# Attention stage: norm parts in other half units, weighing between score tiles where no projection stands, and the loop over images written out

## The chip, the cores and the metric

The kernel runs on one core of a Trainium2 chip. The metric is the device time of one execution in microseconds (us). Five engines matter: PE (TensorE, matmul), DVE (VectorE), ACT (ScalarE), POOL (GpSimd) and SP (SyncE, which here issues every DMA).

## What is computed

The input is 8 images of 384 channels and 32 x 32 pixels. Three stages follow one another: a correlation and 1x1 convolution, an attention over the 1024 pixels of each image, and a feed-forward net. Only the attention is touched:

```
t = t + _L1_attn_ref(_ln_t(t), Wq, Wk, Wv, Wo, bo)

q, k, v = (x @ W.T) split into H = 12 heads of HD = 32
scores  = einsum('bhqd,bhkd->bhqk', q, k) * HD ** -0.5
probs   = softmax(scores, axis=-1)
out     = einsum('bhqk,bhkd->bhqd', probs, v)
return out @ Wo.T + bo
```

`_ln_t` takes mean and variance of a pixel's 384 channels. Weights and activations of the projections are split into two f16 parts (high and low), and a projection is nine matmuls for three products of parts.

## The kernel before, in words

**Order.** `attention_stage` writes one program for each engine, by hand. An image has 24 units (`IU`). Unit u of image b handles one group of 4 heads, a block of 256 queries (x = u // 2) and one half of the keys (kh = u % 2). It has two half units, e = 0 and 1. In a half, PE does four score tiles of 128 x 512 (`scores`, L903), one for each head, into two PSUM banks that alternate; ACT takes the exponential of each (`exponential`, L1237). Tile n waits for exponential n - 2. POOL adds each head's two exponentials of a unit (`add_pair`, L1367). PE then weighs: `weigh` (L934) multiplies the values with the exponentials (16 matmuls of f32) and sums the pairs with a matrix of ones (8 matmuls). It is called behind the fourth tile, and at e = 0 weighs the second half of the unit two before, at e = 1 the first half of the unit before.

**Maxima.** A wave (`wave`, L919) is four row-tiled matmuls into `mx`, four PSUM banks that exist once; DVE reduces it (`take_wave`, L1075). There is one wave at the end of each half, eight waves ahead of its use. After each fourth wave DVE builds the shifts of a block (`top`, `top_turned`, four `shift`), and SP sends them into a row of `qst` (`load_rows`, L764), for which the first score tile of the block waits.

**Beside this**, units 6 to 23 (`FIRST` = 6) of image b hold the 18 projections of image b + 1 (`project`, `project_part`), in pieces of the nine matmuls between the tiles, into one bank `pj`; ACT and DVE stage the results (`stage_high`, `stage_low`). In units 0 to 5 stand the six output projections of image b - 1 (`out_project`, `out_part`, `move_out`, POOL's `add`). When a block's sums are complete, ACT moves them out (`move_pv`), DVE inverts them in three steps (`invert_sum`) and multiplies (`attended`), and ACT and POOL split the result in two.

**Norm** of image b + 2, in units 6 to 23 with `load`: POOL folds (`fold_x`, units 8, 9), PE takes the mean (`mean`, units 10 and 11 = `MEAN_AT`), DVE centres three times for each half of the image (`centre`), ACT squares and POOL folds in units 12 to 15, PE takes the variance (`var`, units 16 and 17 = `VAR_AT`), DVE turns it (`invert_std` step 0), POOL raises it to -0.5 (`invert`), DVE turns it back (step 2) and scales (`normalise`). The two f16 parts are made in units 0 to 2 of the next image (`z_high` on ACT, `z_low` on DVE). `beside(n)` on ACT and DVE says after which exponential, or place n of 8, a part stands; on DVE the waves are taken ahead of n = 0 and 4. A mean or variance matmul uses `pj`, so the units `MEAN_AT + VAR_AT` (10, 11, 16, 17) have their whole projection in the first half, and unit 3 has it in the second.

**Schedule.** `schedule` (L688) gives the order over images. Units 0 to 5 of image 0 stand ahead of a hardware loop `Fori(0, last - 1)` of six turns; its body is units 6 to 23 of image b and units 0 to 5 of image b + 1. Behind it are written out: units 6 to 23 of image 6 (no load) and all of image 7 (units 6 to 23 without projections). SP has the same loop (L811); at the end of its body it waits for the last `add`, stores the image and loads the residual of the next (L818 to L820), ahead of the shifts' rows of the next unit 6.

## Time and profile before

| | |
|---|---|
| median of 3 runs | 2930.32 us (2927.63 to 2931.25) |
| the profiled execution | 2929.51 us |
| its span, first to last instruction | 2927.6 us |
| mean granted TensorE clock | 0.951 |
| PE, busy matmul | 2624.0 us, 90% |
| DVE | 1849.9 us, 63% |
| ACT | 1533.7 us, 52% |
| POOL | 1418.2 us, 48% |
| attention stage, first to last exponential | 474 to 2087 us |
| DMA packets | 68634, 164.41 MB |

Matmuls are pipelined, and a busy share is a mean over three stages with other limits. So what counts here is the attention stage by units: how long a unit takes, which engine is busy for all of it, and where PE stands idle, with the engine that released it. PEclk is the granted clock as a share of 2.4 GHz; 0.5 is 1.2 GHz.

### The profile page before, as it was taken

The numbers are of one execution on the slowest core, as the hardware profiler recorded it, in microseconds if no ns is written. First come the engines' busy times: TensorE is split into PE (matmuls) and PEld (weight loads), VectorE is DVE, ScalarE is ACT, GpSimd is POOL, SyncE is SP. The second block draws the span as 40 slices with busy tenths as digits, with TensorE's granted clock in tenths as the row PEclk, the third lists the DMA queues.
The fourth block names the chain that finished last, engine by engine and source line by source line (L and its number), as shares of the span: only waits on it lengthen the run. The fifth ranks groups of instructions, "written<-read, shape, count | busy, mean of one in ns | idle before, by whom it ended". The sixth has DMA issues, their size and how long they took to land. (4 is left out here: it accounts for less than half of the span.)

```text
span 2927.6 us, 64485 instructions
## 1 busy us (share of the span) xinstructions
PE 2624.0 (90%) x23600; PEld 1287.3 (44%) x23600; DVE 1849.9 (63%) x2359; ACT 1533.7 (52%) x2602; POOL 1418.2 (48%) x1113
## 2 busy tenths in 40 slices
PE   4989756998998998998899999998679999999999
PEld 3555323444453443444444444543234444444444
DVE  6766347887887887797887887777243333333332
ACT  2333124666666665665666666666444444444443
POOL 2333054777776776777766777677511111111010
PEclk8889878999999999999999999999989999999999
DMA  4233132111212112112112112120111010101010
GB/s 153 82 117 110 67 122 84 52 31 50 77 31 95 36 36 92 39 31 96 32 42 96 30 30 74 31 73 2 40 69 43 22 44 21 43 21 43 21 43 22
DMA packets 68634, 164.41 MB, mean 56 GB/s; under 512 B 13569, under 2 KB 17470, under 8 KB 67326
## 3 DMA queue, kind: packets, MB, share of 16 engines
q1 hardware_dynamic: 68350, 160.60, 17.3%
q8 instruction: 181, 2.97, 0.4%
q14 instruction: 103, 0.84, 0.1%
HBM read 59.13 MB, written 37.75 MB: 33 GB/s over the span
## 5 line engine op out<-in xcount | busy, mean ns | idle before, releaser
L1372 POOL TENSOR_TENSOR b_pair<-b_ex 128x512 f32<-128x512 f32 x768 | 979.8, 1301 | 440.4 <-ACT b_ex L1244 439.2
L1244 ACT ACTIVATE b_ex<-b_st 128x512 f32<-128x512 f32 x1536 | 860.3, 597 | 463.6 <-PE b_st L913 445.7
L1079 DVE TENSOR_REDUCE b_mxp<-b_mx 128x4 f32<-128x2048 f32 x384 | 876.6, 2283 | 222.2 <-PE b_mx L929 208.2
L913 PE MATMUL b_st<-b_qst,b_kst 97*128 97x256 f16 (+1 forms) x3072 | 541.3, 280 | 58.8 <-ACT b_ex L1244 35.8
L1628 DVE TENSOR_TENSOR c_gs<-c_g,c_gs 128x512 f16<-128x512 f32 x192 | 132.7, 692 | 481.9 <-ACT c_gs L1701 481.9
L946 PE MATMUL b_pv<-b_ex,b_v 128*32 128x256 f32 x6144 | 420.7, 392 | 0.0
L1549 PE MATMUL c_hid<-c_z,c_wi 128*128 128x512 f16 x1728 | 405.3, 380 | 11.3 <-DVE c_z L1621 11.3
L1564 PE MATMUL c_acc<-c_gs,c_wo 128*128 128x512 f16 x1728 | 404.0, 379 | 0.3 <-DVE c_gs L1628 0.3
L913 PEld LDWEIGHTS b_st<-b_qst,b_kst 97*128 97x128 f16 (+1 forms) x3072 | 226.3, 98 | 367.2 <-ACT b_ex L1244 203.9
L1697 ACT ACTIVATE c_g<-c_hid,c_bias 128x512 f32<-128x512 f32 x192 | 131.3, 684 | 363.6 <-PE c_hid L1549 363.4
L1549 PEld LDWEIGHTS c_hid<-c_z,c_wi 128*128 128x128 f16 x1728 | 169.3, 98 | 227.5 <-issue 19.0
L1564 PEld LDWEIGHTS c_acc<-c_gs,c_wo 128*128 128x128 f16 x1728 | 169.0, 98 | 204.4 <-ACT c_gs L1701 0.8
L1734 POOL TENSOR_TENSOR c_xs<-c_x 128x512 f32<-128x512 f32 x16 | 21.9, 1367 | 477.3 <-DMA c_x<-after_attention 475.0
L954 PE MATMUL b_pv<-b_pair,b_ones 128*32 128x256 f32 x3072 | 240.3, 385 | 0.8 <-POOL b_pair L1372 0.8
L946 PEld LDWEIGHTS b_pv<-b_ex,b_v 128*32 128x32 f32 x6144 | 162.6, 110 | 153.2 <-issue 85.3
L929 PE MATMUL b_mx<-b_kst,b_qst 32*128 32x512 f16 x1536 | 153.4, 389 | 77.6 <-DVE b_mxp L1079 75.8
L929 PEld LDWEIGHTS b_mx<-b_kst,b_qst 32*128 32x128 f16 x1536 | 38.7, 91 | 241.5 <-issue 125.3
L873 PE MATMUL b_pj<-b_z,b_wq 128*128 128x512 f16 x405 | 123.9, 402 | 18.3 <-DVE b_z L1062 11.4
L954 PEld LDWEIGHTS b_pv<-b_pair,b_ones 128*32 128x32 f32 x3072 | 101.2, 112 | 70.2 <-issue 5.0
L1701 ACT ACTIVATE c_gs<-c_g 128x512 f16<-128x512 f32 x192 | 120.9, 629 | 6.1
L897 PE MATMUL b_pj<-b_ao,b_wo 128*128 128x512 f16 x432 | 119.6, 379 | 4.5 <-ACT b_ot L1264 4.5
L308 PE MATMUL a_conv<-a_fs,a_wm 128*128 128x512 f16 x432 | 117.4, 423 | 0.0
(169 smaller groups left out, 2758.5 us busy)
## 6 DMA issues: line engine op xcount, KB each, us to landing
a_x<-in_x SPq DMA_DIRECT2D x8, 1536.0 KB, 6.7
a_ob<-a_x SPq DMA_DIRECT2D x8, 1536.0 KB, 7.1
after_conv<-a_ob SPq DMA_DIRECT2D x24, 512.0 KB, 2.6
b_xl<-after_conv SPq DMA_DIRECT2D x8, 1536.0 KB, 7.3
b_qst<-b_staged0q SPq DMA_DIRECT2D x192, 64.0 KB, 2.0
b_kst<-b_staged0k SPq DMA_DIRECT2D x192, 64.0 KB, 2.0
b_v<-b_vstaged SPq DMA_DIRECT2D x24, 512.0 KB, 3.0
b_xr<-after_conv SPq DMA_DIRECT2D x8, 1536.0 KB, 6.6
```

The lines of the kernel that those rows point to most:

```text
L873: last = nc.tensor.matmul(bank[:, :], ws[kind][a][:, k, g * P:(g + 1) * P], z[b][:, k, part * BANK:(part + 1) * BANK], start=n == 0, stop= ...
L913: last = nc.tensor.matmul(st[n % NST][:, j * QUERIES:(j + 1) * QUERIES], kst[g][0:depth, s, kt * P:(kt + 1) * P], qst[g][0:depth, s, q0:q0 ...
L929: last = nc.tensor.matmul(mx[:, s, :], qst[g][rows, s, q0 + t * P:q0 + (t + 1) * P], kst[g][rows, s, half * BANK:(half + 1) * BANK], start ...
L946: last = nc.tensor.matmul(pv[s * HEAD:(s + 1) * HEAD, 0:QUERIES], v[g][:, kt, s * HEAD:(s + 1) * HEAD], ex[u % 2][e][s][:, j * QUERIES:(j ...
L954: last = nc.tensor.matmul(pv[s * HEAD:(s + 1) * HEAD, QUERIES:BANK], ones[:, :], pair[u % 2][s][:, e * QUERIES:(e + 1) * QUERIES], start=F ...
L1079: nc.vector.reduce_max(mxp[x % 2][:, w // 2, :, w % 2], mx[:, :, :], AX_X).then_inc(mx_taken, 1)
L1244: nc.scalar.activation(ex[u % 2][e][s][:, :], st[n % NST][:, :], ACT.Exp, scale=SCALE).then_inc(exp_ready, 1)
L1372: nc.gpsimd.tensor_tensor(pair[u % 2][s][:, :], ex[u % 2][0][s][:, :], ex[u % 2][1][s][:, :], ALU.add).then_inc(pair_ready, 1)
L1549: last = nc.tensor.matmul(hid[m % NH][:, :], wi[a][:, k, m * P:(m + 1) * P], z[p][b][:, k, :], start=n == 0, stop=n == 8)
L1564: last = nc.tensor.matmul(acc[j][:, :], wo[a][:, m, j * P:(j + 1) * P], gs[m % NS][b][:, :], start=m == 0 and n == 0, stop=m == MC - 1 and ...
L1628: nc.vector.tensor_tensor(gs[m % NS][1][:, :], g[m % NG][:, :], gs[m % NS][0][:, :], ALU.subtract).then_inc(glo_ready, 1)
L1697: nc.scalar.activation(g[m % NG][:, :], hid[m % NH][:, :], ACT.Gelu, bias=bias[:, m:m + 1], scale=1.0 / WSCALE).then_inc(gelu_ready, 1)
```

## The change

On PE, DVE, ACT, POOL and SP the loop over images becomes a loop of the program's text, so that each image is written out. `mean` and `centre` of half 1 move to unit 13, its matmul to the first half unit; which half holds a whole projection is now in `WHOLE` (unit 10: first, 11 and 13: second, 16 and 17: first; 3: second as before). `weigh` is cut in two, `weigh_values` and `weigh_sums`; in a half without a projection the values stand behind the second score tile and the sums behind the third. The steps of `invert_std`, `normalise`, `z_low` and `z_high`, POOL's `invert` and `stage_low` of odd units get other places.

```diff
--- before.py
+++ after.py
@@ -691,7 +691,7 @@
             prologue()
             for u in range(FIRST):
                 unit(0, u, out_proj=False, norm=True)
-            with eng.Fori(0, last - 1) as b:
+            for b in range(last - 1):
                 for u in range(FIRST, IU):
                     unit(b, u, load=True)
                 for u in range(FIRST):
@@ -720,7 +720,10 @@
             return ot if in_prologue(m) else std_turned
 
         V_UNITS = [FIRST + 6 * g + 4 + part for g in range(GROUPS) for part in range(2)]
-        MEAN_AT, VAR_AT = V_UNITS[0:2], V_UNITS[2:4]
+        VAR_AT = V_UNITS[2:4]
+        MEAN_AT = ((V_UNITS[0], 1), (V_UNITS[1] + 2, 0))
+        WHOLE = {V_UNITS[0]: 0, V_UNITS[1]: 1, V_UNITS[1] + 2: 1, VAR_AT[0]: 0, VAR_AT[1]: 0}
+        CENTRE_FROM = (5, 1)
 
         def has_wave(b, h):
             return not (isinstance(b, int) and b == n_images - 1 and h + AHEAD >= WAVES)
@@ -808,7 +811,7 @@
             prologue()
             for u in range(FIRST):
                 unit(0, u)
-            with sp.Fori(0, last - 1) as b:
+            for b in range(last - 1):
                 for u in range(FIRST, IU):
                     unit(b, u)
                     if u == FIRST:
@@ -931,7 +934,7 @@
                                             start=True, stop=True, tile_position=(s * HEAD, 0))
                 last.then_inc(mx_ready, 1)
 
-            def weigh(b, u, e):
+            def weigh_values(b, u, e):
                 x, kh = u // 2, u % 2
                 unit_no = IU * b + u
                 g = x // 4
@@ -949,7 +952,10 @@
                                                 start=kt == 0, stop=False,
                                                 tile_position=(0, s * HEAD))
                 last.then_inc(pv_ready, 1)
-                pe.wait_ge(pair_ready, HG * (unit_no + 1))
+
+            def weigh_sums(b, u, e):
+                kh = u % 2
+                pe.wait_ge(pair_ready, HG * (IU * b + u + 1))
                 for s in range(HG):
                     last = nc.tensor.matmul(pv[s * HEAD:(s + 1) * HEAD, QUERIES:BANK], ones[:, :],
                                             pair[u % 2][s][:, e * QUERIES:(e + 1) * QUERIES],
@@ -986,41 +992,45 @@
                     part = lambda n0, n1: out_part(b - 1, u, n0, n1)
                 if u == FIRST:
                     free[id(pj)] = None
-                first_half = qkv and u in MEAN_AT + VAR_AT
-                second_half = u == KC
+                whole = 1 if u == KC else WHOLE.get(u)
 
                 for e in range(2):
                     scores(b, u, e, 0)
                     scores(b, u, e, 1)
+                    if load and (u, e) in MEAN_AT:
+                        mean(b + 2, MEAN_AT.index((u, e)))
                     pieces = (0, 0), (0, 0)
-                    if first_half or second_half:
-                        if e == second_half:
-                            pieces = (0, 5), (5, 9)
-                    else:
+                    if begin and whole is None:
                         pieces = ((0, 3), (3, 5)) if e == 0 else ((5, 8), (8, 9))
-                    if begin and pieces[0][1]:
+                    elif begin and e == whole:
+                        pieces = (0, 5), (5, 9)
+                    weighed = lagging(b, u, 2 - e) and (*before(b, u, 2 - e), 1 - e)
+                    if pieces[0][1]:
                         if pieces[0][0] == 0:
                             if u == FIRST:
                                 pe.wait_ge(exp_ready, FILLS * (IU * b + u) + 1)
                             begin()
                         part(*pieces[0])
-                    if load and u in MEAN_AT and e == 1:
-                        mean(b + 2, MEAN_AT.index(u))
+                    elif weighed:
+                        weigh_values(*weighed)
                     if load and u in VAR_AT and e == 1:
                         var(b + 2, VAR_AT.index(u))
                     scores(b, u, e, 2)
-                    if begin and pieces[0][1]:
+                    if pieces[0][1]:
                         part(*pieces[1])
+                    elif weighed:
+                        weigh_sums(*weighed)
                     scores(b, u, e, 3)
-                    if lagging(b, u, 2 - e):
-                        weigh(*before(b, u, 2 - e), 1 - e)
+                    if weighed and pieces[0][1]:
+                        weigh_values(*weighed)
+                        weigh_sums(*weighed)
                     if has_wave(b, 2 * u + e):
                         wave(b, 2 * u + e)
 
             def epilogue(b):
-                weigh(b, IU - 2, 1)
-                weigh(b, IU - 1, 0)
-                weigh(b, IU - 1, 1)
+                for u, e in ((IU - 2, 1), (IU - 1, 0), (IU - 1, 1)):
+                    weigh_values(b, u, e)
+                    weigh_sums(b, u, e)
                 for i in range(6):
                     out_project(b, i)
                     out_part(b, i, 0, 9)
@@ -1113,6 +1123,8 @@
                 dve.wait_ge(sum_inverted, INVERSE * (BLOCKS * b + x + 1))
                 nc.vector.tensor_tensor(pvs[:, 0:QUERIES], pvs[:, 0:QUERIES], inv[:, :], ALU.mult
                                         ).then_inc(att_ready, 1)
+
+            NORMALISE = ((18, 6), (19, 1), (19, 2), (20, 6), (21, 1), (22, 5))
 
             def prologue():
                 nc.vector.memset(top[:, :], 0.0).then_inc(const_set, 1)
@@ -1161,26 +1173,24 @@
             def unit(b, u, out_proj=True, norm=True, qkv=True, load=False):
                 def beside(n):
 
-                    if n == 5 and u >= FIRST and qkv:
-                        stage_low(b + 1, u - FIRST)
                     if u % 2 == 0 and n == 1 and lagging(b, u, 4):
                         attended(b, (u - 4) // 2)
-                    if load and u in MEAN_AT and n >= 5:
-                        centre(b + 2, MEAN_AT.index(u), n - 5)
-                    if load and u == VAR_AT[0] and n >= 5:
-                        invert_std(b + 2, 0, n - 5)
-                    if load and (u, n) in ((VAR_AT[1], 5), (VAR_AT[1], 7), (VAR_AT[1] + 1, 2)):
-                        invert_std(b + 2, 1, (5, 7, 2).index(n))
-                    if load and (u, n) in ((18, 3), (18, 6), (19, 1)):
-                        normalise(b + 2, 0, (3, 6, 1).index(n))
-                    if load and (u, n) in ((19, 2), (20, 6), (21, 1)):
-                        normalise(b + 2, 1, (2, 6, 1).index(n))
+                    for h in range(HALVES):
+                        k = n - CENTRE_FROM[h]
+                        if load and u == MEAN_AT[h][0] and 0 <= k < KC:
+                            centre(b + 2, h, k)
+                    if load and (u, n) in ((VAR_AT[0], 5), (VAR_AT[1], 5)):
+                        invert_std(b + 2, 0, 2 * (u - VAR_AT[0]))
                     if u % 2 and n >= 5 and lagging(b, u, 3):
                         invert_sum(b, (u - 3) // 2, n - 5)
-                    if norm and (u, n) in ((0, 6), (0, 7), (1, 1)):
-                        z_low(b + 1, 0, (6, 7, 1).index(n))
-                    if norm and (u, n) in ((1, 7), (2, 2), (2, 3)):
-                        z_low(b + 1, 1, (7, 2, 3).index(n))
+                    if n == (7 if u % 2 else 5) and u >= FIRST and qkv:
+                        stage_low(b + 1, u - FIRST)
+                    if load and (u, n) in ((VAR_AT[1], 7), (VAR_AT[1] + 1, 5)):
+                        invert_std(b + 2, 1, 2 * (u - VAR_AT[1]))
+                    if load and (u, n) in NORMALISE:
+                        normalise(b + 2, *divmod(NORMALISE.index((u, n)), KC))
+                    if norm and u < 2 * KC and n == (1 if u % 2 else 5):
+                        z_low(b + 1, u // KC, u % KC)
 
                 for n in range(8):
                     if n % 4 == 0 and has_wave(b, 2 * u + n // 4 - 1):
@@ -1299,9 +1309,9 @@
                         h, step = u // 2 - 6, u % 2
                         if n in (1, 5) and (step == 0 or n == 1):
                             square(b + 2, h, 2 * step + n // 5)
-                    if norm and u < 2 and n in (1, 3, 5):
-                        z_high(b + 1, u, n // 2)
-                    if qkv and u >= FIRST and n == (2 if u in MEAN_AT + VAR_AT else 6):
+                    if norm and u in (0, 2, 4) and n in (1, 5):
+                        z_high(b + 1, *divmod(u + n // 5, KC))
+                    if qkv and u >= FIRST and n == {None: 6, 0: 3, 1: 7}[WHOLE.get(u)]:
                         stage_high(b + 1, u - FIRST)
                     if u % 2 and n == 3 and lagging(b, u, 3):
                         move_pv(b, (u - 3) // 2)
@@ -1401,8 +1411,8 @@
                 for s in range(HG):
                     if load and u in (8, 9) and s == 1:
                         fold_x(b + 2, u - 8)
-                    if load and (u, s) in ((VAR_AT[0], 3), (VAR_AT[1], 3)):
-                        invert(b + 2, VAR_AT.index(u))
+                    if load and s == 0 and u - 1 in VAR_AT:
+                        invert(b + 2, VAR_AT.index(u - 1))
                     if load and 12 <= u < 16 and s == 3 - u % 2 * 2:
                         fold_square(b + 2, u // 2 - 6, 1 + u % 2)
                     if u % 2 == 0 and s == 3 and lagging(b, u, 4):
```

## Rows read from the trace of the kernel before

**Rows 1.** Waits: engine and line, what it waited for: us, times, longest.

```profile
PE b_mx L929 <- DVE b_mxp L1079: 75.8, 37, 5.8
```

**Rows 2.** Busy us by stretch (columns in the first line); cut at units' first exponentials.

```profile
core 0: us, PE busy (x) PEld busy (x) DVE busy (x) ACT busy (x) POOL busy (x), PEclk, DMA share, GB/s
679.19:709.20 30.01, 24.36 (x245) 11.20 (x244) 25.01 (x26) 17.76 (x33) 23.21 (x19) 0.94 0.21 56
...
716.68:738.50 21.82, 18.18 (x164) 7.84 (x163) 12.34 (x16) 10.75 (x20) 12.98 (x12) 0.84 0.38 143
1757.64:1773.49 15.85, 15.30 (x165) 7.26 (x164) 13.04 (x16) 10.76 (x21) 13.20 (x12) 1.00 0.26 101
761.75:795.53 33.78, 32.45 (x384) 17.25 (x383) 28.77 (x37) 22.58 (x43) 24.93 (x22) 1.00 0.14 41
810.75:863.73 52.98, 48.45 (x546) 25.38 (x545) 46.12 (x59) 32.03 (x61) 40.17 (x31) 0.97 0.16 41
1844.57:1892.09 47.52, 46.22 (x543) 23.98 (x542) 37.23 (x47) 32.00 (x61) 31.64 (x28) 1.00 0.17 46
1628.67:1636.15 7.48, 7.48 (x83) 3.46 (x81) 7.13 (x12) 5.94 (x12) 6.20 (x6) 1.00 0.01 4
1829.30:1836.93 7.63, 7.63 (x83) 3.59 (x82) 7.15 (x12) 5.12 (x10) 4.96 (x5) 1.00 0.01 1
1970.96:2060.62 89.66, 74.09 (x865) 31.54 (x864) 68.03 (x85) 56.86 (x109) 61.83 (x54) 1.00 0.01 2
474.29:522.36 48.07, 36.57 (x360) 14.44 (x360) 39.15 (x46) 30.10 (x58) 29.72 (x24) 0.86 0.04 14
```

**Rows 3.** Timeline of PE, units 5 and 6 of image 1: start, us, line, [idle <-releaser].

```profile
726.38 0.61 PE L913 MATMUL b_st<-b_qst,b_kst 97*128 97x256 f16 x4 [2.58 <-issue]
```

**Rows 4.** Timeline of PE, end of unit 17's first half, image 1.

```profile
825.87 0.39 PE L929 MATMUL b_mx<-b_kst,b_qst 32*128 32x512 f16 x4 [2.64 <-DVE b_mxp L1079]
```

**Rows 5.** Timeline of DVE: image 0 unit 2, image 1 unit 17, image 6 unit 2.

```profile
495.63 1.29 DVE L1062 TENSOR_TENSOR b_z<-b_xl,b_z 128x512 f16<-128x512 f32 x2
...
822.92 0.71 DVE L1050 STREAM_TRANSPOSE b_xs<-b_std_col 128x512 f32<-128x512 f32 x1 [4.10 <-POOL b_std_col L1364]
...
1733.94 3.44 DVE L1062 TENSOR_TENSOR b_z<-b_xl,b_z 128x512 f16<-128x512 f32 x2
```

**Rows 6.** Timeline of POOL: the power for unit 17 of image 1.

```profile
819.97 2.92 POOL L1364 TENSOR_TENSOR b_std_col<-b_std_col,b_power 128x16 f32<-128x16 f32 x1
```

**Rows 7.** Groups by line: busy us, mean ns of one | idle before.

```profile
L1079 DVE TENSOR_REDUCE b_mxp<-b_mx 128x4 f32<-128x2048 f32 x384 | 876.6, 2283 | 222.2 <-PE b_mx L929 208.2 <-issue 13.1
```

**Rows 8.** Timeline of PE, first scores of unit 14: in the loop, written out.

```profile
1628.24 0.61 PE L913 MATMUL b_st<-b_qst,b_kst 97*128 97x256 f16 x4
...
1828.79 0.61 PE L913 MATMUL b_st<-b_qst,b_kst 97*128 97x256 f16 x4
```

**Rows 9.** Timeline of ACT, first exponentials of the same two units.

```profile
1628.67 1.08 ACT L1244 ACTIVATE b_ex<-b_st 128x512 f32<-128x512 f32 x2 [1.00 <-PE b_st L913]
...
1829.30 2.41 ACT L1244 ACTIVATE b_ex<-b_st 128x512 f32<-128x512 f32 x4 [1.00 <-PE b_st L913]
```

**Rows 10.** Timeline of PE, one half unit of the last image.

```profile
2000.33 0.61 PE L913 MATMUL b_st<-b_qst,b_kst 97*128 97x256 f16 x4
2001.49 0.88 PE L913 MATMUL b_st<-b_qst,b_kst 97*128 97x256 f16 x4 [0.55 <-ACT b_ex L1244]
2002.30 1.07 PE L946 MATMUL b_pv<-b_ex,b_v 128*32 128x256 f32 x16
2003.19 0.61 PE L954 MATMUL b_pv<-b_pair,b_ones 128*32 128x256 f32 x8
```

**Rows 11.** Timeline of PE, start of unit 8 of image 6.

```profile
1781.26 0.61 PE L913 MATMUL b_st<-b_qst,b_kst 97*128 97x256 f16 x4 [0.58 <-DMA b_qst<-b_shift]
```

**Rows 12.** DMA queue of instructions: packets, MB; 1098 to 1306 us, then 1750 to 1958.

```profile
q8 instruction: 20, 0.33, 0.7%
...
q8 instruction: 18, 0.29, 0.6%
```

## The prediction

> **What bounds the kernel now.** I read the attention stage alone (474 to 2087 us of the span): the diff touches nothing else. A unit is one pass of the inner order: eight score tiles and exponentials, four pair sums, two waves (the row maxima of a later block, in `mx`, one buffer, emptied by DVE). First the windows by stretch [rows 2], each cut at a unit's first exponential: a steady unit is 7.48 us with PE busy for all of it, so PE bounds it. What exceeds that stands in three places of each image. (1) Units 5 and 6, where the loop over images turns: 21.82 us, against 15.85 where the same units are written out (image 6). (2) Units 1 to 3: 30.0 us. (3) Units 16 to 21: 52.98, against 47.52 in image 6, which loads nothing and so has no norm parts there. Then the waits [rows 1]: PE's wave matmul waits for DVE's reduce, 75.8 us in all. In time order: at the turn PE stands still for 2.58 us with "issue" as the reason [rows 3], so nothing of the program holds it, and the window's clock is 0.84 against 1.00, which makes up the rest of the 6 us. In unit 17 PE waits 2.64 us for a reduce [rows 4]; DVE came late to it because it had waited 4.10 us for POOL's power [rows 5], which took 2.92 us and had been queued behind pair sums [rows 6]. In unit 2 DVE does two `z_low` in a row, 3.44 us [rows 5], between two reduces. Last, the last image: no projection from unit 6 on, and still 89.66/12 = 7.47 us a unit, since the third score tile starts 1.16 us after the first, behind exponential 0 [rows 10].
>
> **Part 1, the loop written out.** Removed: five turns. Each costs 21.82 - 15.85 = 5.97 us [rows 2]; by the same windows the five come to 29. **-29.** Added: straight-line code has its price in rows too. Where units are written out today (images 6, 7), unit 14 takes 7.63, not 7.48 [rows 2]: exponential 0 starts 0.51 us behind the first score matmul (1828.79 to 1829.30) instead of 0.43 (1628.24 to 1628.67) [rows 8, 9], PE's third tile waits for it, twice a unit. I charge +0.15 to each ordinary unit newly written out: units 8, 9, 14, 15, 22, 23 of images 0 to 5, 36 x 0.15 = **+5.4**, and units 0, 4, 5 of images 1 to 6, **+2.7**. A turn also gave the DMAs time. SP stores the image, loads the residual and only then sends the rows of shifts that unit 8 reads; in image 6 PE waits 0.58 us for them [rows 11], beside the 0.15: some 0.8 for unit 7, **+4** for images 1 to 5. No other engine's order changes by this part.
>
> **Part 2, norm parts.** `z_low` goes from units 0 to 2 to one in each of units 0 to 5, `z_high` with it on ACT. DVE's budget for a pair of units there: four reduces at 2.28 [rows 7] 9.1, the shift chain and `attended` 1.8, `invert_sum` 1.2, two `z_low` at 1.4 (between 0.65 alone and 1.72 beside POOL [rows 5]): 14.9 of 15.3. No stretch between two reduces holds more than 1.8, and a reduce may be 1.1 late before PE's next wave waits (half unit 3.8, less 0.4 of wave matmul, less 2.3). So lateness stays inside that cover: I take 0.3 us an image, between 0 and the 6 that are lost today. Units 1 to 3 of images 1 to 6 become 7.63 + 7.63 + 8.0 + 0.3 = 23.6 from 30.0 (six such stretches): 6 x -6.5 = **-39**. (8.0: unit 3 has a half without projection, below.)
> Units 16, 17: DVE's second transpose of the deviation moves from n 7 to n 5 of the next unit, and POOL's power to the head of units 17 and 18. POOL then has about 3 us from the end of the power to DVE's step; that wait goes. What is late next is DVE itself: behind unit 17's second reduce it has the transpose 0.7, `invert_sum` 1.2 and the next transpose and add 1.2, 3.1 us where 1.5 keep pace, and then two or three `normalise` and `stage_low` in 18 to 20. Going from reduce to reduce by hand, PE waits 0.15, 0.35, 0.7, 0.2, 0.3 and 0.4: 2.1 us (bounds 0 and the 5.4 of today). POOL's load in 17 and 18, 5.1 of pair sums, 0.3 and 2.9 each, is 8.3 against 8.9 and 8.0: its pair sums are read a unit later, which hides 0.3. Units 16 to 21: 47.52 as in image 6, written out already [rows 2], + 0.8 for the wait behind the two variance halves (part 3) + 2.1 = 50.4 from 52.98, 6 images: **-15.5**.
> Mean and centre of half 1 move from unit 11 to 13, unit 11 projects in its second half and waits no longer for the centring to free `pj`; unit 13 becomes whole and longer by 1.1. Units 10 to 13: unit 11 loses 1.0 and unit 12 0.4, unit 13 gains 1.1: 33.4 from 33.78 [rows 2], 6 images: **-2**.
> `stage_low` behind `invert_sum` in odd units: nothing, `pj` is asked for 2 us later.
>
> **Part 3, weighing between score tiles** where a half has no projection. In order of PE today such a half is: two tiles, idle until exponential 0, tile, tile, values 0.89 (2002.30 to 2003.19), sums and wave 0.88 [rows 10]: 3.74. Values and sums now fill the idle time: PE's own work is 0.44 + 0.22 + 0.22 + 0.89 + 0.88 and some 0.35 for four changes between f32 and f16, 3.0. But behind tile 3 only the wave and one tile stand ahead of the next half's tile 1, which shares its bank: 0.77 of work against 0.51 + 0.60 + 0.04 for exponential 3, so 0.38 of waiting comes back. A half is 3.4, a unit 6.8 (floor 6.6, the ring through the exponential; ceiling today's 7.47). DVE, 12 us of busy work and 0.5 of gaps a pair, allows 6.5. Last image, units 8 to 19: 12 x 6.8 = 81.6 from 89.66; units 20 to 23 and 3 together -0.7: **-8.7**. Units 6 and 7 there gain nothing, the rows of shifts end them. In the halves with a mean or a variance matmul (0.9) the idle time is already filled, and the order costs them 0.3 by that same wait; that is in the sums above, as is 0.35 gained in units 11 and 3. Image 6, no load: **-1**. Image 0, units 0 to 5: all halves are free, DVE bounds: twelve reduces 27.4, six `z_low` 9, chains 6, gaps 1.5 and the half clock at the start give 45 from 48.07 [rows 2]: **-3**.
>
> **Sum**: -29 + 5.4 + 2.7 + 4 - 39 - 15.5 - 2 - 8.7 - 1 - 3 = -86. The profiled execution took 2929.5 us (span 2927.6 and 1.9 around it): 2843.5. The median of the runs shown is 2930.3, 0.8 above; I forecast **2844**.
>
> **A rule weighed against the trace.** `z_low` is 0.65 in a stretch where POOL has nothing to do, and 1.72 a piece beside pair sums [rows 5]. The Trainium skill (SBUF — State Buffer, on the shared port pair) says that a DVE instruction with two SBUF inputs and a GpSimd instruction that reads SBUF exclude each other: the later one is blocked to the end of the earlier. By that rule a spread `z_low`, always beside a busy POOL, could take up to 1.3 + 0.65 us, and this speaks against the change; by it the sum would be some 10 us higher.
>
> **Rivals.** (A) *DVE remains late*: the spread parts add up, PE waits as long as today. For it: DVE's budget is 97% full in units 0 to 5, the 3.1 us in unit 17. Against it: the longest stretch between two reduces falls from 5.3 (chain and two `z_low`) to 3.1. Time: 2844 + 6 x (6.2 + 3.3) = 2900. (B) *The straight-line price is not paid*, because PE has work ahead in more halves or ACT's waits come out differently: 2844 - 8 - 12 = 2824. (C) *Port*: each `z_low` and `normalise` as long as 1.95: 6 x 1.7 = +10, 2854. (D) *Slower: instructions are not there in time.* Every instruction of five more images comes from memory once. If straight-line PE code stood still for 2.58 us, as at a turn, at each packet of the instruction queue (20 an image in the loop, 18 written out [rows 12]), 5 x 18 pauses would give +232, 3076; at the full 6 us it decides from 15 pauses on. Against it: the loop fetches as many packets today, and images 6 and 7 show 7.63 from unit to unit with no such pause. The Trainium skill (Runtime: NRT & Kernel Launch, Instruction fetch mechanics) says the same: sequential fetch is mostly hidden, a taken branch is not. (E) *No effect*: the gain of the turns is eaten by the row wait in unit 7 (up to 4 us each) and all stalls remain: 2925.
>
> **Chances.** Forecast's case (2820 to 2866) 0.72; A 0.12; B 0.06; C 0.05; D 0.03; E 0.02. Range: down to B, 2820; up by the stalls at half of today's (+28), and the last image unchanged (+8): 2880. Some 0.2% (6 us) is what a measurement can tell: faster 0.95, same 0.02, slower 0.03.
>
> **What would show it.** Right: no "issue" gap of over 1 us on PE between units 5 and 6, and the clock at 1.00 from image 1 to 7; units 1 to 3 near 23.6; no wait of DVE for POOL's power; unit 14 at 7.63; last image's units at 6.8. Wrong: PE's wait for the reduces still above 30 us; pauses named "issue" in straight code; unit 7 above 9.

## The result and the profile after

The changed kernel takes **2832.18 us**, median of 4 runs (2831.3 to 2832.55), the kernel before 2930.78 (2927.63 to 2934.43) beside it: a ratio of 0.9663, 95% interval 0.9646 to 0.9679. The forecast was 2844, range 2820 to 2880, faster: direction, range and most of the size hold. The profiled span fell from 2927.6 to 2830.6 us, by 97.

First the page after: span, busy time by engine, granted clock (PEclk), the instruction queue q8.

```profile
span 2830.6 us, 59176 instructions
...
PE 2625.7 (93%) x23600; PEld 1264.5 (45%) x23600; DVE 1845.6 (65%) x2359; ACT 1539.8 (54%) x2602; POOL 1420.7 (50%) x1113
...
PEclk8899868999999999999999999999799999999999
...
q8 instruction: 163, 2.67, 0.4%
```

The work is the same (PE 2625.7 us busy, 2624.0 before; DVE 1845.6 and 1849.9). Only idle time and clock differ.

Then the windows of after by stretch, cut at units' first exponentials (columns in the first line), each to be laid beside one of [rows 2].

```profile
core 0: us, PE busy (x) PEld busy (x) DVE busy (x) ACT busy (x) POOL busy (x), PEclk, DMA share, GB/s
671.64:694.98 23.34, 23.23 (x245) 10.66 (x244) 21.73 (x23) 17.19 (x33) 22.00 (x18) 1.00 0.25 69
702.61:718.53 15.92, 15.37 (x164) 7.17 (x163) 14.56 (x18) 10.76 (x20) 13.91 (x12) 1.00 0.26 99
751.53:784.34 32.81, 32.37 (x356) 15.71 (x357) 27.41 (x37) 23.36 (x45) 23.40 (x21) 1.00 0.09 27
792.06:841.65 49.59, 48.56 (x547) 24.36 (x546) 44.77 (x58) 32.38 (x61) 39.57 (x31) 1.00 0.17 44
...
1630.77:1638.40 7.63, 7.63 (x83) 3.58 (x82) 6.58 (x11) 6.04 (x12) 4.73 (x5) 1.00 0.30 70
1880.71:1963.04 82.33, 78.47 (x863) 27.51 (x863) 68.21 (x85) 59.31 (x108) 62.14 (x54) 1.00 0.01 2
475.26:517.57 42.31, 37.61 (x358) 12.72 (x359) 39.00 (x44) 31.01 (x57) 29.48 (x24) 0.88 0.04 15
...
517.57:1994.00 1476.43, 1442.37 (x16104) 698.86 (x16108) 1247.34 (x1519) 1019.55 (x1915) 1156.16 (x942) 1.00 0.18 53
```

In the order of the rows: units 1 to 3 of image 1 take 23.34 us (30.01 before), 5 and 6 take 15.92 (21.82), 10 to 13 take 32.81 (33.78), 16 to 21 take 49.59 (52.98), an ordinary unit 7.63 (here unit 0 of image 6), units 8 to 19 of the last image 82.33 (89.66), units 0 to 5 of image 0 42.31 (48.07). The clock is 1.00 where units 1 to 3 had 0.94 and 5 and 6 had 0.84; by the last row it is 1.00 from unit 6 of image 0 to the end of the stage. Of the waits (engine, line, released by: us in all, times, longest), PE's for the reduce fell from 75.8 us [rows 1]:

```profile
PE b_mx L932 <- DVE b_mxp L1089: 18.2, 20, 5.8
```

In both kernels 9.8 us of these lie ahead of the first exponential. In the stage itself the waits fell from 66 us to 8.

The account of the whole stage, first to last exponential, from each unit's first exponential in both traces:

| us, all images together | before to after | forecast |
|---|---|---|
| units 1 to 3, images 1 to 6 | 181.2 to 140.0, **-41.2** | -39 |
| units 5, 6, images 1 to 5 | 108.05 to 79.6, **-28.5** | -29, and +0.9 for unit 5 |
| units 16 to 21, images 0 to 5 | 321.2 to 297.8, **-23.4** | -15.5 |
| units 8 to 19, last image | 89.7 to 82.3, **-7.3** | -8 |
| units 0 to 5, image 0 | 48.1 to 42.3, **-5.8** | -3 |
| image 6, units 6 to 23 | 142.8 to 141.0, **-1.7** | -1 |
| units 10 to 13, images 0 to 5 | 202.7 to 203.3, **+0.6** | -2 |
| ordinary units of images 0 to 5, and units 0, 4 | **+3.1** and **+1.9** | +5.4 and +1.8 |
| unit 7, images 0 to 5 | **+4.0** | +4 |
| units 20 to 23 of the last image | **+1.5** | -0.3 |

### The profile page after: what moved, and what is told of

Same layout as the page of the kernel before. It is cut to its first block and busy times, and to the rows that moved or that the text cites. A ratio compares the mean times of both kernels' runs of the same rounds, so it can differ in the third digit from the quotient of the medians.

```text
span 2830.6 us, 59176 instructions
## 1 busy us (share of the span) xinstructions
PE 2625.7 (93%) x23600; PEld 1264.5 (45%) x23600; DVE 1845.6 (65%) x2359; ACT 1539.8 (54%) x2602; POOL 1420.7 (50%) x1113
## 5 line engine op out<-in xcount | busy, mean ns | idle before, releaser
L1254 ACT ACTIVATE b_ex<-b_st 128x512 f32<-128x512 f32 x1536 | 869.9, 598 | 407.8 <-PE b_st L916 374.2
L916 PE MATMUL b_st<-b_qst,b_kst 97*128 97x256 f16 (+1 forms) x3072 | 548.3, 277 | 22.0 <-ACT b_ex L1254 8.3
L949 PE MATMUL b_pv<-b_ex,b_v 128*32 128x256 f32 x6144 | 411.9, 386 | 1.9 <-ACT b_pvs L1262 1.7
L916 PEld LDWEIGHTS b_st<-b_qst,b_kst 97*128 97x128 f16 (+1 forms) x3072 | 216.0, 97 | 370.4 <-ACT b_ex L1254 200.7
L932 PE MATMUL b_mx<-b_kst,b_qst 32*128 32x512 f16 x1536 | 152.6, 387 | 19.8 <-DVE b_mxp L1089 18.2
L876 PE MATMUL b_pj<-b_z,b_wq 128*128 128x512 f16 x405 | 115.3, 385 | 14.9 <-DVE b_z L1072 11.4
L960 PEld LDWEIGHTS b_pv<-b_pair,b_ones 128*32 128x32 f32 x3072 | 90.8, 110 | 70.9 <-issue 15.2
L524 POOL TENSOR_TENSOR a_sqs<-a_sq 128x1024 f32<-128x1024 f32 x8 | 18.8, 2352 | 202.9 <-ACT a_sq L502 202.9
L876 PE MATMUL b_pj<-b_z,b_wk 128*128 128x512 f16 x405 | 115.8, 380 | 2.2 <-DVE b_staged0q L1082 2.2
```

What stands on the lines that cost most here:

```text
L876: last = nc.tensor.matmul(bank[:, :], ws[kind][a][:, k, g * P:(g + 1) * P], z[b][:, k, part * BANK:(part + 1) * BANK], start=n == 0, stop= ...
L916: last = nc.tensor.matmul(st[n % NST][:, j * QUERIES:(j + 1) * QUERIES], kst[g][0:depth, s, kt * P:(kt + 1) * P], qst[g][0:depth, s, q0:q0 ...
L932: last = nc.tensor.matmul(mx[:, s, :], qst[g][rows, s, q0 + t * P:q0 + (t + 1) * P], kst[g][rows, s, half * BANK:(half + 1) * BANK], start ...
L949: last = nc.tensor.matmul(pv[s * HEAD:(s + 1) * HEAD, 0:QUERIES], v[g][:, kt, s * HEAD:(s + 1) * HEAD], ex[u % 2][e][s][:, j * QUERIES:(j ...
L960: last = nc.tensor.matmul(pv[s * HEAD:(s + 1) * HEAD, QUERIES:BANK], ones[:, :], pair[u % 2][s][:, e * QUERIES:(e + 1) * QUERIES], start=F ...
L1254: nc.scalar.activation(ex[u % 2][e][s][:, :], st[n % NST][:, :], ACT.Exp, scale=SCALE).then_inc(exp_ready, 1)
```

## Experiments

Ratios are to the kernel before, run on the same chip. "After +" names an edit of the changed kernel, "before +" one of the old.

**1. The loop alone.** Before + both loops over images written out:

```diff
-            with eng.Fori(0, last - 1) as b:
+            for b in range(last - 1):
```

> The kernel before with the loop over images written out on the five engines and nothing else. My sum has five turns at 29 us less, 0.15 us a unit more in the 144 units that are newly written out (of which some 60 wait for something else anyway), and 4 us of waiting for the rows of shifts: 17 us less in all, 2914. In the trace: no PE gap named issue at units 5 and 6, unit 14 of image 3 at 7.63 instead of 7.48, units 1 to 3 still 30.1 us, units 16 to 21 still 53. Rival, straight-line code costs nothing and only images 6 and 7 are slow for a reason of their own: 2901, unit 14 at 7.48.

Measured: 2911.12 us, ratio 0.9930 (0.9911 to 0.9949). Nearer to my 2914 than to the rival's 2901. The turns are gone, the ordinary unit costs 7.63. But units 16 to 21 of images 0 to 5 take 328.1 us, 7 more than in the loop: the old order of parts leaves no cover, and what the straight line adds falls on the path. That last clause is my reading; no run isolates it. In image 1 unit 18 alone went from 9.44 to 11.21 us and unit 19 from 7.48 to 9.18. Either way the parts of the change are not additive.

**2. The loop kept.** After + both `Fori` back.

> The changed kernel with the hardware loop over images put back on the five engines. Theory: the five turns come back at 5.8 us each, +29, and the units in the loop run at 7.48 instead of 7.63, some 14 units of 6 images, -13: 2848. The half clock is back behind each turn. Rival, the turns are covered once DVE is less behind: 2820, faster than the changed kernel.

Measured: 2849.48, ratio 0.9723 (0.9704 to 0.9742): as the theory said (2848), and the rival (2820) is out. Timeline of PE, unit 5 into 6 of image 1 (start, us, line, idle before and its releaser), as [rows 3] but longer:

```profile
710.45 1.03 PE L916 MATMUL b_st<-b_qst,b_kst 97*128 97x256 f16 x4 [2.89 <-issue]
```

Units 5 and 6 of images 1 to 5 take 108.4 us against 79.6 written out: 5.8 us a turn. Ordinary units are back at 7.48. Written out is worth 17 us net here: 29 of turns, less the straight-line price and the row wait.

**3. The straight-line price.** After + another order of ACT's three waits ahead of an exponential:

```diff
+                act.wait_ge(st_ready, FILLS * unit_no + n + 1)
                 if lagging(b, u, 2):
                     act.wait_ge(pv_ready, 2 * (unit_no - 2) + e + 1)
                     act.wait_ge(pair_ready, HG * (unit_no - 2) + s + 1)
-                act.wait_ge(st_ready, FILLS * unit_no + n + 1)
```

In the built program of straight code the first wait stays on the exponential, and the others become a semaphore instruction ahead of it. In the old order the wait for the score tile, which comes last, stood on that instruction, and the exponential had still to follow; in the new one it stands on the exponential itself. The trace of after has such an instruction of ACT's sequencer (ACTq) of 38 ns ahead of nearly every exponential; ahead of the one shown below it stands at 1549.87:

```profile
L1253 ACTq EVENT_SEMAPHORE  x1520: 38/38/38, 490.0 to 1990.2; - x190
```

> The changed kernel with one change in the exponential: it waits for its score tile first in the program's order, and for the weighing and the pair sum of two units ago after it. Theory: of several waits on constants the build leaves the first on the ACTIVATE and puts the rest on an instruction of their own ahead of it; today that one holds the tile's semaphore, the last to come, and the ACTIVATE starts 0.08 us later than in the loop, where waits on registers are set up apart. With the order turned, exponential 0 starts 0.43 us behind the first score matmul, an ordinary unit takes 7.48 again, 0.15 less in some 150 units, and the ring through exponential 3 in the last image is 0.08 shorter a half: -24, 2808. Rival, the 0.08 us is a property of straight-line code on ACT or PE: 2832, unit at 7.63.

Measured: 2813.09, ratio 0.9595 (0.9579 to 0.9612): 19 us faster by one moved line, where I had expected 24. Unit 14 of image 5, PE's first scores and ACT's first exponential, after:

```profile
1549.44 0.50 PE L916 MATMUL b_st<-b_qst,b_kst 97*128 97x256 f16 x3
...
1549.95 1.08 ACT L1254 ACTIVATE b_ex<-b_st 128x512 f32<-128x512 f32 x2 [1.00 <-PE b_st L916]
```

and with the tile's wait first:

```profile
1535.94 0.61 PE L916 MATMUL b_st<-b_qst,b_kst 97*128 97x256 f16 x4
...
1536.37 1.08 ACT L1254 ACTIVATE b_ex<-b_st 128x512 f32<-128x512 f32 x2 [1.00 <-PE b_st L916]
...
1536.37:1543.85 7.48, 7.48 (x83) 3.45 (x81) 6.41 (x11) 5.94 (x12) 5.28 (x5) 1.00 0.01 1
```

From score to exponential it is 0.43 us again instead of 0.51, as in the loop [rows 8, 9], and the unit 7.48. The price that I had read as one of straight code is one of the waits' order: 0.08 us, twice a unit.

**4. Weighing behind the fourth tile** everywhere. After + `weigh_values` and `weigh_sums` together at the old place.

> The changed kernel with values and sums weighed behind the fourth tile in every half, as before. Theory: the last image's units 8 to 19 go from 6.86 back to 7.47, +7.3; image 0's first six units +3 to +5; units 3 and 11 +0.35 each, +4; the halves with a mean or a variance matmul get back 0.3 each, -7; 2840. Rival, the sums that come earlier in all halves release ACT's move and POOL, and this is what shortened units 16 to 21: 2850 or more, with units 16 to 21 above 51.

Measured: 2842.45, ratio 0.9695 (0.9677 to 0.9713), near the theory (2840); units 16 to 21 did not get longer, so the rival is out. The net loss is 10 us against the changed kernel: the last image's units 8 to 19 take 91.2, image 0's first six 48.1. PE in the last image waits for the exponential in every half:

```profile
1924.90 0.61 PE L916 MATMUL b_st<-b_qst,b_kst 97*128 97x256 f16 x4
1926.06 0.88 PE L916 MATMUL b_st<-b_qst,b_kst 97*128 97x256 f16 x4 [0.55 <-ACT b_ex L1250]
```

and in after, the same place, the values fill the gap:

```profile
1921.22 0.90 PE L916 MATMUL b_st<-b_qst,b_kst 97*128 97x256 f16 x4
1922.05 1.07 PE L949 MATMUL b_pv<-b_ex,b_v 128*32 128x256 f32 x16
1923.05 0.39 PE L916 MATMUL b_st<-b_qst,b_kst 97*128 97x256 f16 x2
1923.38 0.64 PE L960 MATMUL b_pv<-b_pair,b_ones 128*32 128x256 f32 x8
```

But units with a mean or variance matmul got shorter (16 and 17: 8.49 each from 8.80 and 9.09; 13: 8.68 from 9.02), so there the new place costs: 4.2 us in units 16 to 21 and 2.0 in 10 to 13 of images 0 to 5 (293.6 and 201.3).

**5. The z parts together.** After + `z_low` and `z_high` at their old places in units 0 to 2.

> The changed kernel with z_high and z_low back in units 0 to 2, all else as changed. Theory: two z_low in a row behind the shift chain make DVE late by 5.3 us, PE waits at a wave in unit 2 and falls to the half clock: units 1 to 3 from 23.3 to some 29.5, 6 images, and +2 in image 0: +39, 2871. Rival, DVE is bound in units 0 to 5 by its sum, so that a spread costs as much and the gain came from the loop: units 1 to 3 within 25, 2840.

Measured: 2870.95, ratio 0.9802 (0.9786 to 0.9819). Units 1 to 3 of images 1 to 6 take 176.2 us for 140.0. The theory (2871) holds. DVE in unit 2 of image 1, then PE:

```profile
682.56 1.54 DVE L1104 TENSOR_SCALAR b_shift<-b_top_turned 8x32 f16<-8x32 f32 x4
684.13 1.38 DVE L1124 TENSOR_TENSOR b_pvs<-b_pvs,b_inv 128x256 f32<-128x256 f32 x1
685.44 3.43 DVE L1072 TENSOR_TENSOR b_z<-b_xl,b_z 128x512 f16<-128x512 f32 x2
688.80 2.28 DVE L1089 TENSOR_REDUCE b_mxp<-b_mx 128x4 f32<-128x2048 f32 x1
...
691.13 0.61 PE L932 MATMUL b_mx<-b_kst,b_qst 32*128 32x512 f16 x4 [4.92 <-DVE b_mxp L1089]
```

Shifts, `attended` and two `z_low` are 6.4 us of work between two reduces; PE stands 4.92 us, and the stretch of units 1 to 3 has a clock of 0.89 again (0.94 before, 1.00 after). So of the 7.4 us that image 1 loses here, some 2.5 aren't the wait itself but the half clock behind it. This is the largest single part of the gain.

**6. The power waited for.** After + `invert_std` and POOL's `invert` at their old places.

> The changed kernel with DVE's steps of invert_std and POOL's power back in their places of before (DVE's second step in the same unit as the first, POOL's power ahead of the last pair sum), all else as changed. Theory: DVE waits 4 us for the power again, units 16 to 21 go from 49.6 to 54 or 55 in 6 images: +29, 2861. Rival, what bounds these units is DVE's 3.1 us behind unit 17's second reduce and the scalings behind it, and the wait for the power only stands in front of that: +10, 2842.

Measured: 2843.42, ratio 0.9708 (0.9692 to 0.9724). My theory (2861) missed, and the rival's size is right. DVE and PE in unit 17 of image 1:

```profile
805.16 0.71 DVE L1060 STREAM_TRANSPOSE b_xs<-b_std_col 128x512 f32<-128x512 f32 x1 [4.13 <-POOL b_std_col L1374]
...
808.10 0.40 PE L932 MATMUL b_mx<-b_kst,b_qst 32*128 32x512 f16 x4 [1.97 <-DVE b_mxp L1089]
```

DVE waits as long as before [rows 5], but PE loses only 1.97 us and units 16 to 21 lose 2.0 an image (309.7 for 297.8 in six), not the 5 that I had ascribed to it. The mean hides two cases: images 1 to 4 lose 1.4 each, images 0 and 5 lose 3.1, because a part of their unit 17 ran at half clock (12.76 and 12.70 us against 11.0 to 11.1, at the same wait).

**7. The scaling early**, alone and with 6. After + the old list of places:

```diff
-            NORMALISE = ((18, 6), (19, 1), (19, 2), (20, 6), (21, 1), (22, 5))
+            NORMALISE = ((18, 3), (18, 6), (19, 1), (19, 2), (20, 6), (21, 1))
```

> The changed kernel with the six normalise back in their places of before (units 18 to 21, one place earlier each, two behind the shift chain of unit 18), all else as changed. The run with the power waited for again cost only 11 us where I expected 29, so the step from 55.2 us for units 16 to 21 (loop written out alone) to 51.1 must lie in the other moves. Theory: the scalings' places carry it: with them back, a scaling behind the shift chain in unit 18 makes that stretch 2.6 us and PE waits some 1.5 to 3 us an image more: +9 to +18, 2845. Rival, it needs both at once, DVE late from the power and the scaling on top: +2, 2834.

Measured: 2833.14, ratio 0.9670 (0.9653 to 0.9686): no change. My theory (2845) missed, the rival (2834) is right. With 6 as well:

> Both back: the power waited for, and the scalings in their places of before. Theory (the two add up, and stage_low's place and the weighing between tiles carry nothing): units 16 to 21 at 55 again, 6 x 5.5 = +33, 2865. Rival, part of the difference is the mean and variance halves or stage_low: 53 or less, 2853.

Measured: 2851.9, ratio 0.9732 (0.9712 to 0.9751). Units 16 to 21: 297.8 after, 309.7 with the power, 297.8 with the scaling, 318.1 with both. The scaling costs nothing alone and 8.4 us on top of the power. But 3.3 of the 8.4 stand in unit 17, ahead of the first scaling, and are clock alone. Unit 17 of image 1, with the power, then with both (columns as in the windows of after):

```profile
801.86:812.98 11.12, 9.04 (x110) 5.00 (x111) 7.25 (x9) 5.67 (x10) 8.53 (x7) 1.00 0.23 55
```

```profile
804.64:817.40 12.76, 10.68 (x110) 5.40 (x111) 7.37 (x9) 5.67 (x10) 8.51 (x7) 0.87 0.20 48
```

PE waits 1.97 and 1.96 us there. The longer form fell in two images with the power alone and in four with both. The other 5.1 us, 0.8 an image, are the scaling's, behind unit 17: with both, PE waits for reduces some 0.5 us in unit 18 and 0.2 in unit 19; with the power alone it has no wait there, with the scaling alone 0.15 and 0.2, and after has 0.4 in unit 19. So I read it that lateness of DVE is free up to some cover, and a second piece counts once a first has used it up. How large the cover is no run measures; my 1.1 us a reduce stays an estimate. The total with both lies 1 us below the rival and 13 below my theory.

**8. `stage_low` early**, alone and with both. After + `stage_low` at place 5 of every unit but 13, ahead of the row sums' inversion; then with 6 and 7.

> The changed kernel with stage_low moved back: it stands half a unit early again, at half unit n 5 ahead of the attended piece and of the row sums' inversion, in every unit but 13. The power and the scaling stay at their new places. My theory, that the waits of units 16 to 21 come only once VectorE has lost more than about 1.1 us of cover, and that one place moved back is not enough when the power is early: no change, 2832 us, units 16 to 21 of images 0 to 5 at 298 us together. The rival, that stage_low standing ahead of the attended piece makes the row sums' inversion late by itself: about 0.8 us in each of six images, 2837 us, with the loss in unit 17 or 18.

Measured: 2831.42, ratio 0.9664 (0.9647 to 0.9680), units 16 to 21 at 295.8: no change that can be told.

> The changed kernel with power, scaling and stage_low all at their old places; the halves of mean and variance, the z parts, the weighing and the written out loop stay new. Power and scaling together left units 16 to 21 of images 0 to 5 at 318.1 us, and the kernel with the written out loop alone has 328.1. My theory, that stage_low's place carries the remaining 10 us: 326 to 328 us in these units, 2861 us in all, with DVE's wait for the power at 38 us or more. The rival, that the rest lies in the new places of the weighing and of the mean and variance halves: 318 us in these units and 2852 us in all.

Measured: 2848.98, ratio 0.9720 (0.9704 to 0.9736), units 16 to 21 at 316.2, as the rival said: `stage_low` isn't the missing piece. Of the 12 us to the 328.1 of experiment 1, units 18 are most: 11.21 there in images 1 to 4, 8.39 to 8.42 here. Units 19 add 5 us, and units 16, 17 and 21 give 5 back. PE's wait for the reduce in unit 18 is 3.51 us there and 0.5 here, and behind it a part of unit 19 runs at half clock in images 1 to 4 (image 1 of experiment 1; here this unit has 7.87 at 1.00):

```profile
837.78:846.96 9.18, 9.18 (x83) 4.09 (x82) 7.50 (x9) 5.54 (x10) 3.06 (x3) 0.81 0.18 66
```

DVE at the head of unit 18 of image 1, first in the kernel with the loop alone, then with all three parts back:

```profile
829.78 1.74 DVE L1094 TENSOR_SCALAR b_shift<-b_top_turned 8x32 f16<-8x32 f32 x4
831.55 1.45 DVE L1114 TENSOR_TENSOR b_pvs<-b_pvs,b_inv 128x256 f32<-128x256 f32 x1
```

```profile
817.74 0.78 DVE L1104 TENSOR_SCALAR b_shift<-b_top_turned 8x32 f16<-8x32 f32 x4
818.55 0.42 DVE L1124 TENSOR_TENSOR b_pvs<-b_pvs,b_inv 128x256 f32<-128x256 f32 x1
```

The same five instructions take 3.19 and 1.20 us. POOL in the first case is at its pair sums, in the second at the end of its power:

```profile
830.19 5.61 POOL L1372 TENSOR_TENSOR b_pair<-b_ex 128x512 f32<-128x512 f32 x4
```

```profile
815.71 2.91 POOL L1374 TENSOR_TENSOR b_std_col<-b_std_col,b_power 128x16 f32<-128x16 f32 x1
```

So 2.0 us of the 2.8 are DVE beside another POOL instruction. Why the two kernels fall into these different alignments, and whether that is the whole of the 12 us, no run isolates; it stays open. Of what still differs between them, the place of the weighing in the second halves of units 16 and 17 lies inside this stretch; all three parts back with the weighing behind the fourth tile would be the run to tell, and it was not made.

**9. The rows' wait.** After + the residual's load on SP put behind unit 6's rows of shifts:

```diff
                     if u == FIRST:
+                        if b:
+                            load_r(b)
                         load_x(b + 2)
```

(and it is taken away behind the store; the last two images alike).

> The changed kernel with one thing moved on SP: the residual of the next image is loaded behind the rows of shifts of unit 6, not ahead of them. Theory: PE's wait at unit 8 for these rows (4.0 us in all, and 8.00 and 8.41 in the last image's units 6 and 7, where 6.8 would do) goes; unit 7 is 7.63 in all images: -5, 2827. Rival, the rows still queue behind the store of the image, which is issued just before them: 2832.

Measured: 2826.84, ratio 0.9652 (0.9636 to 0.9668): 5 us faster. In after unit 7 took 7.63 to 9.13, and PE stood before unit 8, here in image 5:

```profile
1499.74 0.61 PE L916 MATMUL b_st<-b_qst,b_kst 97*128 97x256 f16 x4 [1.43 <-DMA b_qst<-b_shift]
```

With the small rows ahead of the 1.5 MB load, unit 7 is 7.63 in images 0 to 5 and 6.73 in the last. What the rows had stood behind is more than the load. The residual goes into the tile that the store reads, so SP, which works in order, waits until the store has landed (issued at 1486.06, landed at 1492.90 in after) and only then issues the residual and the rows; here in image 5 of after, then of this run:

```profile
1486.06 0.39 SPq L822 DMA_DIRECT2D after_attention<-b_xr  x1
1492.91 0.38 SPq L745 DMA_DIRECT2D b_xr<-after_conv  x1
1493.33 1.36 SPq L772 DMA_DIRECT2D b_qst<-b_shift  x2
```

```profile
1482.51 0.39 SPq L824 DMA_DIRECT2D after_attention<-b_xr  x1
1483.14 1.92 SPq L772 DMA_DIRECT2D b_qst<-b_shift  x2
```

The rows landed at 1499.69 in after, 0.4 us behind the residual, and at 1488.23 here, 1.2 us ahead of the store. How much of the gain is SP's wait and how much the place in the queue, this run doesn't part.

**10. A better version.** After + 3 + 9 + the old weighing place in the halves with a mean or variance matmul only:

```diff
-                    elif weighed:
+                    elif weighed and not normed:
                         weigh_values(*weighed)
```

(the sums, and the place behind the fourth tile, alike).

> The changed kernel with the tile's wait first in the exponential (-19 measured), the rows of shifts ahead of the residual on SP (-5 expected), and values and sums behind the fourth tile again in the halves that hold a mean or a variance matmul (10 second, 13 first, 16 and 17 second half), where the first series shows them 1.4 us an image shorter that way: -8. Sum 2800. Rival: shorter halves leave DVE later, so that units 16 to 21 stay at 49.5 and the last gain is under 2: 2806.

Measured: **2803.35 us** (2801.76 to 2804.32), ratio 0.9569 (0.9553 to 0.9585), faster than both kernels. Units 16 to 21 take 291.3, 10 to 13 200.3, the last image's 8 to 19 80.6. Over after it gains 28.8 us: 19.1 by 3, 5.3 by 9, and some 4 that are left for the weighing, where I had expected 8 and the rival under 2.

## Why the prediction held, and where it didn't

**The turns** (-29, +5.4, +2.7): right. Experiments 1 and 2 give 5.7 and 5.8 us a turn. The straight-line price of 0.15 us was measured right, but I charged it to too many units: 9 and 15 were no steady units before (8.29 and 7.74 us), and they didn't get longer (8.20 and 7.71), so +5.4 came out as +3.1. Its cause I had wrong: I took it as given by straight code, while experiment 3 shows it is the wait order of one instruction. Rival B (2824) asked for "ACT's waits come out differently"; they don't by themselves, but one line makes them.

**The row wait** (+4): right in sum, from one row. It is irregular, from none to 1.5 us, and experiment 9 shows it is removable. One of my signs of being wrong, unit 7 above 9, did appear, in one image (9.13 in image 5).

**Units 1 to 3** (-39, measured -41.2): right. The budget between two reduces was the argument, and experiment 5 gives 36.2 of the 41.2 back by undoing this one part (the loop alone is worth 1.4 in these units, the weighing in unit 3 2.1). The cover held; I had taken 0.3 us an image of lateness, there is none (7.63, 7.63, 8.07).

**Units 16 to 21** (-15.5, measured -23.4): the mis-sized term, in two places. I took image 1's 52.98 us for every image, while the mean of the six is 53.5: image 4 has 55.7, with a wait of PE of 4.6 us in unit 18 where image 1 has 1.9. That is 3.3 of the 7.9. The other 4.6 are the 2.1 us of waits "by hand": by the same sum they came out as 1.3 (49.6 less 47.52 and 0.8). The step that failed in the mechanism is that "the 5.4 of today" are all counted as PE's waits. In image 1 PE's waits are 2.64 and 1.89; the rest is clock. Unit 17 before, in image 1 and in image 4, with PE waiting 2.64 and 2.63 us:

```profile
819.16:831.85 12.69, 10.05 (x112) 5.79 (x111) 7.60 (x9) 5.54 (x11) 10.02 (x8) 0.87 0.24 58
1442.11:1453.22 11.11, 8.48 (x112) 5.19 (x111) 6.81 (x6) 5.54 (x11) 8.50 (x7) 1.00 0.28 66
```

A part at 1.2 GHz costs 1.6 us on top of the wait, in five of the six images in unit 17, and it goes with the wait. "That wait goes", said of the power, was right. Before, DVE waited ten times for it, 38.3 us, six of them in the units 17, 4.1 us each. After there are four:

```profile
DVE b_xs L1060 <- POOL b_std_col L1374: 13.8, 4, 4.6
```

and all four lie ahead of the stage, between 402 and 466 us, where they were before too. What I couldn't see in one trace is how little of it is the power's own: by experiments 6 and 7 it is worth 2.0 us an image and power and scaling together 3.4, of the 5.0 that separate experiment 1 from after. The rest lies in alignments that my hand count had no means to see (experiment 8).

**Units 10 to 13** (-2, measured +0.6): unit 11 lost the 1.0 and unit 12 the 0.4 of the forecast, but unit 13 gained 1.3 (8.04, 9.51 and 7.72 for units 12, 11 and 13 in experiment 1; 7.63, 8.52 and 9.02 after) and unit 10, which I had left out, 0.2. Both are halves with a mean matmul, where the values stand in a gap already filled; experiment 4 puts this order at 2.0 us in these units and 4.2 in 16 to 21, 0.17 and 0.35 a half where I had named 0.3. It was near the right size, and missing from this line of the sum (whose own parts give 33.5, not the 33.4 that I wrote).

**The last image** (-8 of the -8.7): measured -7.3 for units 8 to 19, and the mechanism is shown by experiment 4. A unit takes 6.47 to 7.02, mean 6.86, forecast 6.8. Units 20 to 23 went the other way by 1.5 us: the last exponentials end later, though the weighing behind them is 1.0 us shorter.

**Image 0, units 0 to 5** (-3, measured -5.8): under-sized. I had summed 42.4 us of work for DVE; it is busy 39.00 us after, and had been 39.15 before, in a row that I had [rows 2]. The row of the busy time was better than my count of parts.

**Port.** Spreading does make a `z_low` longer, but far less than rival C has it. The 48 of them by line, after and in experiment 5, where they stand together and all else is the same (columns: busy us, mean ns of one, idle before):

```profile
L1072 DVE TENSOR_TENSOR b_z<-b_xl,b_z 128x512 f16<-128x512 f32 x48 | 59.6, 1249 | 0.1
```

```profile
L1072 DVE TENSOR_TENSOR b_z<-b_xl,b_z 128x512 f16<-128x512 f32 x48 | 48.0, 1030 | 0.1
```

Spread out a piece takes 0.22 us more. In the loop, before, the grouped ones took 1424 ns. What differs is how many of the stage's 42 meet an idle POOL: 12 in experiment 5 (0.68 us each), 3 before, 1 after. The longest after is 1.75 us, and a `normalise` takes 0.87 on the mean, so rival C (1.95 each) is out. The row of experiment 8 (3.19 us for what takes 1.20) shows DVE losing time where POOL is at its pair sums. The Trainium skill (SBUF — State Buffer, on the shared port pair) speaks of a lock between the two engines; the trace agrees that they slow each other, but not that each spread part pays the full 1.3 us.

**Rivals A, D, E.** DVE late as today: no, 18.2 us of waits in all, 8 in the stage. Pauses at instruction packets: q8 has 163 packets against 181 and PE has no gap named "issue" of a microsecond in the stage (the one of 1.4 us lies in the first stage and was there before, at 1.3). No effect: no. The result lay 12 us below the forecast. Gains under-sized by 7.9 in units 16 to 21, 2.8 in image 0, 2.2 in units 1 to 3, 0.7 in image 6, 0.4 at the turns and a straight-line price too high by 2.2 make 16.2; against them stand 2.6 in units 10 to 13 and 2.5 in the last image. That leaves 11.1 of the span.

## What to carry to other kernels

Count the work that an in-order engine has between two instructions on which the bounding engine waits, not its total load: spreading six small operations brought 36 us at unchanged busy time. As experiments 6 and 7 read, such lateness costs nothing below the cover and every piece counts above it, so the worth of one edit depends on which others are made. When a wait of the matmul engine goes, look at the granted clock of the same stretch too: part of the gain may be there, and it differs from image to image at equal waits. And when an unrolled loop shows a small constant price, look at the order of the waits and of the queue before accepting it: two small edits gave back 24 us.

## What the runs showed of the hardware

- A wait that stands on an own semaphore instruction ahead of the exponential adds 0.08 us between score and exponential; as the last to arrive it cost 19 us over the kernel.
- A loop's back edge cost PE 2.58 to 3.15 us of standing still (five turns each in before and in experiment 2) and some 3 us more, most of it at half clock. After, where the turns are gone and PE's longest wait is 1.88 us, the clock is 1.00 (2.4 GHz) from unit 6 of image 0 to the end of the stage.
- The same wait of PE can be followed by half clock or not: 12.69 us at 0.87 and 11.11 at 1.00 for unit 17 before, behind 2.64 and 2.63 us.
- Small DVE instructions lose time beside POOL's pair sums and not beside its power: four shifts of 8x32 took 1.74 us beside the sums and 0.78 beside the power, `attended` 1.45 beside the sums and 0.42 as the power ended. Over the stage after, 86 `attended` with POOL idle and six beside the power took 0.42 to 0.43 us, the three beside pair sums 0.89 to 1.51.
